# Moving one subtraction per tile, the low part of the rotated keys, from VectorE to GpSimd in a paged attention kernel on one Trainium2 core

## The reference

```python
q, k, v = x @ Wq.T, x @ Wk.T, x @ Wv.T       # 32 query heads, 8 key heads, 128 wide
q, k = rope(rmsnorm(q, q_norm_w), pos), rope(rmsnorm(k, k_norm_w), pos)
k_all = concat([k_cache[block_table], k])     # 512 cached keys, then the 32 new ones
v_all = concat([v_cache[block_table], v])
probs = softmax(where(valid, q @ k_all.T * SCALE, -1e30))
x = x + (probs @ v_all) @ Wo.T
```

## Time and profile before

| | |
|---|---|
| median of 3 runs | 2198.85 us (2198.59 to 2199.64) |
| the profiled execution | 2200.81 us |
| its span, first to last instruction | 2198.7 us |
| PE busy | 2112.5 us, 96% |
| DVE busy | 1740.5 us, 79% |
| ACT busy | 1481.4 us, 67% |
| POOL busy | 1246.8 us, 57% |
| mean granted TensorE clock | 0.991 of full speed |

### The profile page before, as it was taken

The page is one execution under the profiler, slowest core; times in us unless marked ns, Lnnn a source line. Parts: engine busy times, 40 slices in busy tenths (PEclk is TensorE's granted clock), DMA queues, the critical chain, the costliest instruction groups (busy, mean ns, idle before and its releaser), DMA issues.

```text
span 2198.7 us, 60484 instructions
## 1 busy us (share of the span) xinstructions
PE 2112.5 (96%) x17634; PEld 1373.9 (62%) x17634; DVE 1740.5 (79%) x3933; ACT 1481.4 (67%) x4966; POOL 1246.8 (57%) x2070
## 2 busy tenths in 40 slices
PE   6979889999999999999998999999999999999998
PEld 2435566666666666666665666666666666666665
DVE  8976588888888888888886777788877878777785
ACT  4834567777777777777775666666767766666664
POOL 7011256666666666666664666666666666666663
PEclk9989999999999999999999999999999999999999
DMA  8987587888888888888898686667666676676663
GB/s 229 333 274 255 170 205 202 218 222 227 237 216 221 229 213 227 224 218 222 213 278 212 177 261 191 179 189 181 181 181 179 180 199 182 174 195 182 179 187 102
DMA packets 553804, 458.70 MB, mean 209 GB/s; under 512 B 127861, under 2 KB 482500, under 8 KB 552710
## 3 DMA queue, kind: packets, MB, share of 16 engines
q1 hardware_dynamic: 433062, 295.67, 48.4%
q0 software_dynamic: 40960, 134.25, 19.9%
q10 hardware_dynamic: 79456, 24.91, 7.0%
HBM read 377.21 MB, written 56.70 MB: 197 GB/s over the span
## 4 chain that ended last, share of the span: by engine, by line
PE 74%; DVE 8%; issue 2%; ACT 1%; SPq 1%; DMA 1%; DVEq 0%; ACTq 0%
PE PR L1330 17%; PE WOp L1363 15%; PE Op L1311 13%; PE Sp L1277 13%; PE PTp L1288 10%; DVE split L1577 2%; PE TRp L1340 2%; PE Sp L1280 1%; DVE masked L1530 1%; PE Op L1293 1%; PE Op L1313 1%; DVE qr L1571 1%; DVE pts L1535 1%; DVE rs_ L1572 1%; DVE vn L1586 1%
## 5 line engine op out<-in xcount | busy, mean ns | idle before, releaser
L736 POOL DMA_INDIRECT pages<-values_split,rows x512 | 521.1, 1018 | 121.9 <-issue 108.9
L1330 PE MATMUL PR<-Wt,xT 128*128 128x512 f16 x2232 | 538.0, 379 | 0.0
L1414 ACT ACTIVATE pts<-PTp 128x512 f16<-128x512 f32 x512 | 305.7, 597 | 343.6 <-PE PTp L1288 341.4
L1311 PEld LDWEIGHTS Op<-pts,pages 128*128 128x128 f16 x6144 | 385.6, 98 | 129.3 <-DVE OT L1548 9.7
L1311 PE MATMUL Op<-pts,pages 128*128 128x128 f16 x6144 | 427.3, 219 | 9.8 <-DVE OT L1548 7.2
L1277 PE MATMUL Sp<-pages,qT 128*128 128x512 f16 x1536 | 417.0, 380 | 6.7 <-PEq L183 6.7
L1535 DVE TENSOR_TENSOR pts<-PTp,pts 128x512 f16<-128x512 f32 x512 | 351.5, 686 | 73.9 <-ACT pts L1414 73.8
L1530 DVE CUSTOM_DVE_ANT_0 masked<-Sp,mask 128x544 f32<-128x544 f32 x512 | 370.1, 723 | 47.9 <-PE Sp L1280 41.0
L1420 ACT ACTIVATE masked<-masked,small 128x544 f32<-128x544 f32 x512 | 379.7, 742 | 20.9 <-DVE small L1530 17.6
L1363 PE MATMUL WOp<-WoT,OT 128*128 128x512 f16 x1536 | 378.2, 379 | 0.0
L1288 PE MATMUL PTp<-ident,masked 128*128 128x128 f32 x2048 | 325.3, 281 | 14.5 <-DVE pts L1535 14.5
(11 more groups left out here) (252 smaller groups left out, 2971.9 us busy)
## 6 DMA issues: line engine op xcount, KB each, us to landing
pages<-keys_transposed SPq DMA_DIRECT2D x2048, 64.0 KB
mask<-mask_rows SPq DMA_DIRECT2D x128, 128.0 KB
v<-new_values SPq DMA_DIRECT2D x96, 128.0 KB
weights_split<-wsrc SPq DMA_DIRECT2D x40, 256.0 KB
keys_transposed<-pages SPq DMA_DIRECT2D x32, 256.0 KB, 5.4
values_split<-pages SPq DMA_DIRECT2D x16, 512.0 KB, 5.0
rope_s<-rope_table SPq DMA_DIRECT2D x32, 256.0 KB
pages<-values_split,rows POOLq DMA_INDIRECT x512
```

The source lines that it names most:

```text
L736: nc.gpsimd.indirect_dma_start(out=vS[:, n % 2, c, :, :].rearrange("p l n -> p (l n)"), out_offset=None, in_=v_d, in_offset=bass.IndirectO ...
L1311: nc.tensor.matmul(o, vS[:, par, c, low, h * D:(h + 1) * D], pts[:, u % 2, part, c * P:(c + 1) * P], start=(k == 0), stop=False)
L1330: m = nc.tensor.matmul(bank(k), xT[:, c, xl, :], Wp[:, c, wl, GROUP_COL[k]:GROUP_COL[k] + HID], start=(i == 0), stop=(i == NPASS - 1))
L1414: nc.scalar.activation(pts[:, u % 2, 0, :], PTp[:, :], ACT.Copy).then_inc(G.pt_hi, 1)
```

## The change

The subtraction of group 0 leaves `rotated_low` on DVE. POOL gets it as a function `keys_low`, called in slot 6 behind `add_rotated`. The wait for `split_high` and the signal `split_low` go with it. The DVE list now skips the slot whose `turned` entry is group 0; the ACT list does not change.

```diff
@@ TILE_PLAN
-    squares={1: 0, 3: 1, 6: 3, 8: 4, 10: 5}, values=5, values_low=6,
+    squares={1: 0, 3: 1, 6: 3, 8: 4, 10: 5}, values=5, values_low=6, keys_low=6,
@@ DVE
                     def rotated_low(ti, tt, k):
-                        if k == 0:
-                            v.wait_ge(G.split_high, ti + 1)
-                            V.tensor_tensor(split[:, 1, :], qr[:, norm_no(ti, k) % 2, :], split[:, 0, :], ALU.subtract).then_inc(G.split_low, 1)
-                            return
                         v.wait_ge(G.tr_hi, turn_no(ti, k) + 1)
@@
-                            if sl in plan["turned"]:
+                            if plan["turned"].get(sl, 0) != 0:
                                 rotated_low(ti, tt, plan["turned"][sl])
@@ POOL
+                    def keys_low(ti):
+                        g.wait_ge(G.split_high, ti + 1)
+                        nc.gpsimd.tensor_tensor(split[:, 1, :], qr[:, norm_no(ti, 0) % 2, :], split[:, 0, :], ALU.subtract).then_inc(G.split_low, 1)
+
@@
                             add_rotated(ti, plan["add"][sl])
+                        if ti in proj and sl == plan["keys_low"]:
+                            keys_low(ti)
```

## The result

| | before | changed |
|---|---|---|
| median of 6 runs | 2199.24 us (2196.83 to 2201.26) | 2182.97 us (2179.66 to 2184.12) |
| ratio | | 0.9924, 95% interval 0.9911 to 0.9937 |
| profiled execution | 2200.81 us | 2179.66 us |
| its span | 2198.7 us | 2177.6 us |

The change saves 16.3 us between the medians; the ratio says 0.76%, and its interval 14 to 20 us. The forecast was 19.5 us less, 2179.4 us, in a range from 2176 to 2186. The profiled execution of the changed kernel happens to be the shortest of its six; against its own pair the gain is 21.2 us, so the two profiles alone would flatter the change.

A forecast was written before the change was run, and what follows sets the result against it. PE was taken to bound the kernel, losing time only where it waits for DVE. 18.3 us (tiles 1 to 30) plus 1.2 us (tile 0) gave 19.5 us off, a median of 2179.4 us, range 2176 to 2186.

The forecast's parts named there:

- 0.61 us per tile: Slot 7, tiles 1 to 30: PE's lost time before the transposes of the probabilities, all gained, 18.3 us in total.
- the 30 waits: PE's transposes of the probabilities wait for DVE's low part once in each of tiles 1 to 30; these must go.
- the link in the chain: L1577, the DVE subtraction taken away, 1.57 us between the maxima and L1586 in the waits ahead of PE's transposes.
- POOL's subtraction: The moved 128x512 subtraction on POOL, between the addition and `root`, taken as 1.27 us like the addition.
- the upper bound of 4.6 us: POOL's subtraction if every nanosecond of the 286 ns row over 32 columns grew with the columns.
- L1541 in slot 7: DVE's `normalise` of unit 6, held until POOL's subtraction ends, would last about 1.2 us.
- in hand before `values`: DVE's `o_low` would end 1.2 us before PE needs it for `values` of unit 4.
- in hand before the scaling: POOL's `root` would end 0.6 us before ACT asks for it in `scale_heads`.
- The sum of 19.5 us: Total gain forecast: 18.3 us in tiles 1 to 30 plus 1.2 us in tile 0.
- tiles 0, 14 and 15: Tiles where waits for transfers or the single longer wait might take back up to 2.4 us of gain.
- Rival 1: POOL's subtraction slow: L1541 held, PE stalls from X = 2.47 us, slower than before from 3.1 us; chance 4%.
- Rival 3: Part of the gain returns through transfers in tiles 0, 14, 15 (2182 us) or slots 7 to 9 (2189); chance 13%.

The follow-up runs named there:

- e2_behind: Kernel before, with the subtraction kept on DVE but two places later, behind the low parts of new values and probabilities: 2197.93 us, ratio 0.9942.
- e3_narrow: Kernel before, with DVE's subtraction in its old place over 8 of 512 columns, the rest set to zero: 2199.71 us, ratio 0.9954.
- e11_thrice: Changed kernel with the subtraction done three times on POOL, each waiting for the one before: 2192.38 us, ratio 0.9967 against the kernel before.
- e4_long2: Changed kernel with one more POOL subtraction, 1024 columns wide, ahead of the real one: 2212.87 us, ratio 1.0011 against the kernel before.
- e1_again: Changed kernel, unaltered, run once more against the kernel before on the same chip: 2193.81 us, ratio 0.9924.
- e12_before: Kernel before, unaltered, run once more against itself for another trace: 2217.87 us, ratio 0.9999.

## Why the prediction was right

- **PE bounds the kernel, and 0.61 us per tile is what it loses.** Right: the tile is 0.61 us shorter where nothing else disturbs, and the 30 waits are gone. The gain per tile was 0.61 us, not the 1.57 us of the link in the chain.
- **L1577 is long because it meets POOL's addition.** Shown: 684 ns out of its way (e2_behind), 1124 ns at 8 columns in its way (e3_narrow). The rule of the Trainium skill, "SBUF — State Buffer", section "Who interferes with whom", says that the second comer is blocked for the whole instruction of the first. The traces agree (1617.85 against 1617.83 in e3_narrow), and e11_thrice adds that the waiting engine gets its turn between two instructions of the other.
- **POOL's subtraction: 1.27 us taken, 1.16 measured.** By that, the root ended later by 0.2 instead of 0.3 us. The estimate from the addition of the same size was good; the upper bound of 4.6 us from the 32-column row was never near.
- **L1541 in slot 7: 1.2 us predicted, 1.13 measured;** in hand before `values` 1.2 predicted, 1.4 measured; in hand before the scaling 0.6 predicted, 0.57 measured.
- **The sum of 19.5 us was 2 to 3 us too large.** The four comparisons of the two kernels gave 16.3 to 17.7 us. Both of its terms are found at their places, 0.61 us in slot 7 of each of the tiles 1 to 30 and 1.21 us in slot 6 of tile 0. What the sum left out is that some of it comes back elsewhere. The prediction named tiles 0, 14 and 15 for that, with 2.4 us; 19.5 less 2.4 is 17.1, which fits, but the traces neither show the exchange in tile 0 nor tell it from the scatter. That the total came out inside the range is in part due to a range that allowed for such a loss.
- **Rival 1, POOL too slow, had the wrong place.** It put the first loss at L1541 in slot 7 from X = 2.47 us. By the runs, POOL's time reaches PE through the root of group 4 and ACT in slots 9 to 11: at 3.4 us (2.14 + 1.24, e4_long2) the gain is gone, and at 3.6 us in three pieces (e11_thrice) 6 of 16 us are left. So no single X decides; that the predicted price for slower than before, 3.1 us, lies near the 3.4 of e4_long2 is luck, since the path was another: I had stopped following POOL's queue at the first root, while the gathers carry the backlog on. The bound on DVE itself was not reached, since the longest single hold tried was 2.14 us.
- **Rival 3** fits the size of what came back (2 to 3 us). Its place, the transfers of tiles 0, 14 and 15, is not shown.

## What to carry to other kernels

An instruction that takes 1.65 us where its like takes 0.68 is waiting for something: look at what the neighbouring engine runs at that moment before moving work. Here two places later on the same engine brought most of the gain, and the move to GpSimd was free only because the hold that it puts on VectorE falls into slack. Count the gain by what the bounding engine loses, and expect some of it back where that engine waits for other things: here 2 to 3 of 19.5 us. To say where, the stretches must differ by more than they scatter from one trace of the same kernel to the next. For the room of a moved step, follow the receiving engine's queue until it is idle again, not only to its next taker.

## What the runs showed of the hardware

- A GpSimd subtraction of float16 from float32 into float16 over 128x512 takes 1.16 us (31 times, 1157 to 1169 ns), less than the addition with float32 throughout, 1.27 us; over 1024 columns 2.14 us.
- The hold works in both directions and by single instructions: DVE's 8 columns took 1.12 us under POOL's addition; POOL's 32 columns took 0.57 instead of 0.24 us under DVE's subtraction; DVE's normalising of 544 columns took 0.50, 1.13 or 2.10 us with none, 512 or 1024 columns on POOL, and 1.13 with three times 512 in a row, each waiting for the one before.
- The issue of a transposing transfer from ACT stands in ACT's queue for 1.25 us as a rule (median of 31), 3.4 us at most (e1_again). In some traces of either kernel ACT's next work starts 2.4 us and more after the start of the issue (up to 4.0 in e12_before); what holds it is not shown.
